# Spreading the side jobs of an attention loop anew over its 44 steps: one core, five engines, one table

## What is computed

```python
def xattn(x, context, Wq, Wk, Wv, Wo, bo):
    q, k, v = x @ Wq.T, context @ Wk.T, context @ Wv.T      # 16 heads of 16
    scores = einsum('bhqd,bhkd->bhqk', q, k) * SCALE
    probs = softmax(where(causal, scores, -inf))
    return (probs @ v) @ Wo.T + bo
x = x + tanh(g_xattn) * xattn(layernorm(x), ctx, ...)
x = x + tanh(g_ffn) * experts(layernorm(x), ...)            # top 128 of 512 tokens for each expert
```

## Time and profile before

| | |
|---|---|
| median of 3 runs | 1907.35 us (1906.61 to 1908.03) |
| the profiled execution | 1905.62 us |
| its span | 1903.9 us |
| PE busy | 1772.4 us, 93% |
| DVE, ACT, POOL busy | 1079.0 us, 930.5 us, 931.3 us |
| granted TensorE clock, mean | 0.975 |

### The profile page before, as it was taken

The page is one execution under the profiler, slowest core; times in us unless marked ns, Lnnn a source line. Parts: engine busy times, 40 slices in busy tenths (PEclk is TensorE's granted clock), DMA queues, the critical chain, the costliest instruction groups (busy, mean ns, idle before and its releaser), DMA issues.

```text
span 1903.9 us, 40685 instructions
## 1 busy us (share of the span) xinstructions
PE 1772.4 (93%) x12902; PEld 1017.8 (53%) x12902; DVE 1079.0 (57%) x3480; ACT 930.5 (49%) x1812; POOL 931.3 (49%) x1026
## 2 busy tenths in 40 slices
PE   3899999999999999935899999999899999999997
PEld 1355555555555555422465656565556565656565
DVE  2778888888888887737634343434343434343431
ACT  2466666666666666632334343434343434343332
POOL 6477777777777776543333232333322323333322
PEclk8899999999999999967999999999999999999999
DMA  5777777777777787347464644556736555555222
GB/s 161 163 172 188 189 188 188 188 188 188 188 188 188 188 189 168 81 132 177 100 132 84 120 98 89 98 90 122 123 61 121 100 89 98 89 97 82 48 34 23
DMA packets 408333, 247.85 MB, mean 130 GB/s; under 512 B 289303, under 2 KB 389759, under 8 KB 408191
## 3 DMA queue, kind: packets, MB, share of 16 engines
q1 hardware_dynamic: 383183, 212.39, 47.7%
q0 software_dynamic: 24576, 33.57, 11.3%
q10 hardware_dynamic: 432, 0.13, 0.0%
HBM read 118.63 MB, written 58.72 MB: 93 GB/s over the span
## 4 chain that ended last, share of the span: by engine, by line
PE 50%; DVE 3%; DMA 1%; issue 1%; ACT 0%; POOL 0%; SPq 0%; POOLq 0%; DVEq 0%
PE bank L1101 11%; PE bank L1102 11%; PE bank L1103 11%; PE bank L1117 6%; PE bank L1119 6%; PE bank L1118 6%; DVE h L1219 0%; DVE h L1222 0%; DVE top_at L1169 0%; ACT h L1147 0%; DVE work L1172 0%; DVE top L1167 0%; DMA rows<-tokens,row_now 0%; DMA out<-y,row_now 0%; POOL out L1067 0%
## 5 line engine op out<-in xcount | busy, mean ns | idle before, releaser
L1067 POOL DMA_INDIRECT out<-y,row_now x128 | 202.5, 1582 | 606.6 <-ACT y L1154 581.7
L681 DVE CUSTOM_DVE_ANT_0 masked<-bank,causal 128x128 bf16<-128x128 f32 (+3 forms) x1024 | 445.6, 484 | 69.1 <-PE bank L453 68.2
L565 ACT ACTIVATE prob<-bank 128x512 f32<-128x512 f32 x640 | 367.6, 596 | 158.1 <-PE bank L473 86.1
L1219 DVE TENSOR_TENSOR h<-bank,silu 128x512 f32<-128x512 f32 x256 | 176.4, 689 | 393.5 <-PE bank L1103 259.8
L1147 ACT ACTIVATE h<-h 128x512 bf16<-128x512 f32 x256 | 161.2, 630 | 345.4 <-DVE h L1219 328.5
L1117 PE MATMUL bank<-downT,h 128*128 128x256 bf16 x1024 | 279.1, 273 | 0.0
L1119 PE MATMUL bank<-downT,h 128*128 128x256 bf16 x1024 | 279.1, 273 | 0.0
L1118 PE MATMUL bank<-downT,h 128*128 128x256 bf16 x1024 | 279.1, 273 | 0.0
L1222 DVE TENSOR_TENSOR h<-h 128x512 bf16<-128x512 f32 x256 | 177.3, 692 | 179.7 <-ACT h L1147 175.5
L453 PE MATMUL bank<-ks,qs 96*128 96x128 bf16 (+3 forms) x1024 | 257.8, 306 | 21.0 <-DMA ks<-k_parts 11.4
L1101 PE MATMUL bank<-tokT,gateT 128*128 128x512 bf16 x512 | 195.0, 381 | 35.7 <-DMA tokT<-rows 28.9
(11 more groups left out here) (141 smaller groups left out, 2702.7 us busy)
## 6 DMA issues: line engine op xcount, KB each, us to landing
q_parts<-q_sb SPq DMA_DIRECT2D x64, 192.0 KB, 2.9
k_parts<-k_sb SPq DMA_DIRECT2D x64, 192.0 KB, 3.8
qs<-q_parts SPq DMA_DIRECT2D x64, 192.0 KB, 3.0
ks<-k_parts SPq DMA_DIRECT2D x64, 192.0 KB, 3.2
x_t<-in_x SPq DMA_DIRECT2D x16, 512.0 KB, 4.2
ctx_t<-in_ctx SPq DMA_DIRECT2D x16, 512.0 KB, 4.9
qs<-q_parts SPq DMA_DIRECT2D x64, 128.0 KB, 2.9
ks<-k_parts SPq DMA_DIRECT2D x64, 128.0 KB, 3.2
```

The source lines that it names most:

```text
L565: nc.scalar.activation(prob[:, gr % 2, h0:h0 + nh, POFF[tiles[0]]:POFF[tiles[0]] + w], sc_bank[SC_BANK[k]][:, 0:nh * w].rearrange("p (h w) ...
L681: last = nc.vector.tensor_tensor_reduce(masked[:, (gr * NMAX + k) % 2, part], max_bank[max_at(gr, k)][:, part], causal[:, T - w:T], 1.0, L ...
L1067: nc.gpsimd.indirect_dma_start(out_rows, bass.IndirectOffsetOnAxis(ap=row_now[:, par, c, s:s + 1], axis=0), y[:, c % 2, s, :], None, compu ...
```

## The change

The table `extra` in `steps` is written anew: the same jobs, with the same batch offsets, in other steps and in another order inside a step. Nothing else is changed: no instruction of the arithmetic, no shape, no buffer and no semaphore. `JOB_BANK` follows the order of the jobs, so a few jobs use the other of the two banks. Two of the 30 lines that go and 3 of the 36 that come, those that the prediction speaks of most:

```diff
@@ -85,36 +85,42 @@
 
 
     extra = {
...
-            9: [("pv", b - 1, 2, 3), ("xs", b - 2), ("ln2+", b - 2, 1)],
-            10: [("pv+", b - 1, 2), ("ln2+", b - 2, 0)]},
...
+            8: [("k", b + 1, 0, 0), ("ln2+", b - 2, 1), ("pv", b - 1, 2, 2)],
+            9: [("xs", b - 2), ("ln2+", b - 2, 0), ("pv", b - 1, 2, 3)]},
+        2: {1: [("pv+", b - 1, 2), ("k+", b + 1, 0), ("k", b + 1, 0, 1)],
...
```

More of the change, by code:

```diff
@@ L105, in steps @@
[L105 to L117, removed]
+        0: {0: [("mrow", b - 1, 3)],
+            1: [("ln1+", b + 1, 0), ("yt+", b - 1, 0), ("pv", b - 1, 1, 0), ("yt", b - 1, 0)],
+            2: [("xsplit", b + 1, 0)],
+            3: [("mt", b - 1, 3), ("ln1+", b + 1, 1), ("xturn", b + 1), ("xsplit", b + 1, 1), ("pv", b - 1, 1, 1), ("pv", b - 1, 1, 2)],
+            4: [("csplit", b + 1, 0), ("o", b - 2, 0, 0), ("o", b - 2, 0, 1), ("mt+", b - 1, 3)],
+            5: [("cturn", b + 1)],
+            6: [("o+", b - 2, 0), ("o", b - 2, 1, 0)],
+            7: [("csplit", b + 1, 1), ("o", b - 2, 1, 1), ("pv+", b - 1, 1), ("pv", b - 1, 1, 3), ("o+", b - 2, 1)],
+            9: [("yt", b - 1, 1)]},
@@ new lines, in steps @@
+        1: {0: [("qstack", b, 2), ("kstack", b, 2)],
+            1: [("yturn", b - 1, 0), ("yt+", b - 1, 1), ("mrow", b, 0), ("ysplit", b - 1, 0)],
+            2: [("mt", b, 0), ("mt+", b, 0), ("ln2", b - 2, 0)],
+            3: [("ln2", b - 2, 1), ("pv", b - 1, 2, 0), ("q", b + 1, 0, 0)],
+            4: [("q+", b + 1, 0), ("q", b + 1, 0, 1), ("q", b + 1, 1, 0)],
+            5: [("pv", b - 1, 2, 1)],
+            6: [("q", b + 1, 1, 1), ("kstack", b, 3), ("q+", b + 1, 1)],
+            8: [("k", b + 1, 0, 0), ("ln2+", b - 2, 1), ("pv", b - 1, 2, 2)],
+            9: [("xs", b - 2), ("ln2+", b - 2, 0), ("pv", b - 1, 2, 3)]},
@@ new lines, in steps @@
+        2: {1: [("pv+", b - 1, 2), ("k+", b + 1, 0), ("k", b + 1, 0, 1)],
+            2: [("mt", b, 1), ("mt+", b, 1)],
+            3: [("load", b + 2), ("pv", b - 1, 3, 0)],
+            4: [("k", b + 1, 1, 0), ("k", b + 1, 1, 1), ("k+", b + 1, 1)],
+            5: [("qstack", b, 3), ("yt", b - 1, 2), ("yt+", b - 1, 2), ("pv", b - 1, 3, 1)],
+            7: [("pv", b - 1, 3, 2), ("qstore", b + 1), ("vaug", b)],
+            8: [("pv+", b - 1, 3), ("mrow", b, 1), ("pv", b - 1, 3, 3), ("xt", b - 2, 0), ("xt+", b - 2, 0)],
+            9: [("res", b - 1), ("xt+", b - 2, 1)],
+            10: [("xt", b - 2, 1)]},
@@ new lines, in steps @@
+        3: {0: [("kstore", b + 1)],
+            1: [("mt+", b, 2), ("yt", b - 1, 3), ("yt+", b - 1, 3), ("qstack", b + 1, 0), ("mt", b, 2)],
+            3: [("ll+", b - 2), ("pv", b, 0, 0), ("ll", b - 2), ("v", b + 1, 0, 0), ("kstack", b + 1, 0)],
+            4: [("v+", b + 1, 0), ("v", b + 1, 0, 1), ("ln1", b + 2, 0), ("mrow", b, 2)],
+            5: [("ysplit", b - 1, 1), ("save", b - 2), ("lt", b - 2), ("yturn", b - 1, 1)],
+            6: [("kstack", b + 1, 1), ("v", b + 1, 1, 0), ("lt+", b - 2)],
+            8: [("v", b + 1, 1, 1), ("pv", b, 0, 1), ("v+", b + 1, 1)],
+            9: [("pv+", b, 0)],
+            10: [("ln1", b + 2, 1), ("pv", b, 0, 2), ("qstack", b + 1, 1), ("pv", b, 0, 3)]},
```

## The result

| | before | changed |
|---|---|---|
| median of 6 runs each, on the same chip | 1906.98 us (1905.86 to 1908.39) | 1873.25 us (1872.32 to 1877.36) |
| ratio, 95% interval | | 0.9827 (0.9814 to 0.9839) |
| span of the profiled execution | 1903.9 us | 1871.2 us |
| DVE, ACT, POOL busy | 1079.0, 930.5, 931.3 us | 1075.4, 932.2, 931.7 us |
| granted TensorE clock, mean | 0.975 | 0.974 |

The changed kernel is 33.7 us faster, 1.7%. The forecast was 1874. The other engines do the same work in the same time (DVE's and ACT's busy times move by 0.3% and 0.2%), so the gain lies in PE's time, above all in its waits, as argued. PE's own busy time can't be compared over the whole span: 64 of its records, all in the experts, are missing from the second trace. Whether the terms were right is another matter: several were not, and that they cancelled to within 1 us is luck.

What follows compares the result with a forecast made beforehand. PE sets the pace in the attention, with 3.0 us of waits a batch. 1905.6 less 36 over fifteen batches plus 2.5 at the start gives 1872, or 1874 on the scale of the median; range 1862 to 1900.

Steps and rivals of the forecast that it cites:

- three signs of being wrong: Period over 46.5, PE waiting for `ks` or `qs` in mid-attention, or the start losing over 5 us.
- PE's waits by starts: Attention: a batch of 47.7 us holds 44.7 us of PE work, so 3.0 us are waits; eleven places sum to 3.1.
- Rival 2: Attention: the busy row is right, PE idles only 2.5%, so the time is 1889 or more; chance 0.05.
- Period 45.2: Attention, per batch: 44.7 us of work, less 0.2 for `pv` pairs, plus 0.7 of new waits.
- g0 k5, 0.57 go: `sc` at g0 k5 waits 0.57 us for ACT behind an `ln1+` pair; moving `ln1+` to k1 and k3 removes it.
- g1 k8 to g2 k2: ACT makes `sc` late, 0.71 us, partly seen at `max`; `ln2+` in g1 k8, k9 and `pv+` at g2 k1 remove it.
- g2 k8 to g3 k2, 0.50 go: ACT is late for `sc` behind `xt+`, `pv+`, `xt+`; with PE's jobs moved, the 0.50 us wait goes.
- `pv` pairs, 0.09 each: Two pairs of `pv` now adjacent each save PE one entry of 0.09 us, 0.2 a batch.
- The SP chain has 0.9 of slack: `csplit`, `cturn`, stacks, `yturn`, `mrow` on SP's queue: `mrow` lands at 21.9, PE wants it at 22.8; slack unchanged at 0.9.
- Rival 4: Slower: late `csplit` makes SP's chain set g2; at 4 us of slip 1922; chance 0.07.
- 15 batches at the full 2.4: Attention: 2.4 to 2.5 us saved in each of fifteen batches at the full pattern, 36 us.
- The start loses 2.5: First 85 us, PE waits for DMA: SP's new order costs between 0 and 5 us, taken as 2.5.

Runs made afterwards that it cites:

- m_best: a_mrow with `yt` of group 1 at g0 k10 and `pv` 2.2 beside `pv` 2.3 at g1 k9; 1856.83 us, ratio 0.9736.
- b_ln12: b_ln2 with both `ln1+` pairs of group 0 also moved, to k1 and k3 from k2 and k4; 1904.16 us, ratio 0.9974.
- m_ln: a_mrow with `ln1+`, `ln2+` and `pv+` back where the kernel before has them; 1877.66 us, ratio 0.9837.
- b_ln2: Kernel before with only the `ln2+` pairs moved to g1 k8 and k9 and `pv+` to g2 k1; 1910.46 us, ratio 1.0011.
- m_lnk: m_ln with the first part of the `k` projection back in g2 k1 too; 1872.75 us, ratio 0.9817.
- a_mrow: Changed kernel with `mrow` of group 0 ahead of `yturn` and that of group 1 ahead of q's store on SP's queue; 1859.98 us, ratio 0.9746.
- b_k: b_ln12 with the first `k` part at g1 k8 instead of g2 k1 and `cturn` ahead of the stacks; 1902.12 us, ratio 0.9976.
- a_split: Changed kernel with `mt` of group 3 between the two `pv` of g0 k3 instead of ahead of them; 1873.66 us, ratio 0.9819.
- a_csplit: Changed kernel with the second `csplit` moved from g0 k7 to k9, delaying the SP transfers behind it; 1909.36 us, ratio 1.0006.

## Why the prediction was right, and where it was wrong

The direction is right, and so is the mechanism: waits of PE that go when the side jobs are moved. That the time is right to 1 us is luck, since terms of several us each were off and cancelled. One of its three signs of being wrong came true: PE waits for `qs` in the middle of the attention. By its own steps:

- *PE's waits by starts*, 3.0 to 3.1 a batch: 3.18, and 47.7 as period: 47.75. Right, and the largest part of the gain, 1.84 of 2.45 a batch, is these waits. Rival 2, the busy row, is refuted: it capped the gain at 1889, and the changed kernel ran 1873, m_best 1857. The Trainium skill, "Perfetto Trace Analysis", Identifying the Most-Contended Engine, holds matmul busy time for no measure of headroom. This case agrees: 97.5% busy hid 3.2 us of waits in 47.75, 6.7%.
- *Period 45.2*: 45.3. Right as a sum. Its two parts are each off by half a microsecond and cancel: waits left 0.7 forecast, 1.34 measured; work saved 0.2 forecast, 0.6 measured.
- *g0 k5, 0.57 go*: 0.57 to 0.16 at g0 k4. The size is right, the cause only half: b_ln12 shows that moving `ln1+` alone removes the wait, and m_ln that the new places of the other jobs remove it as well, with `ln1+` where it was. In the new table the move of `ln1+` wins nothing; the 0.15 at g0 k4 stands only with it.
- *g1 k8 to g2 k2, "0.71 go" by the split of `ln2+`*: the wait went (0.69 to 0.36, and the 0.36 is the `mrow`), but **the cause was mis-booked**. b_ln2 shows that the split alone wins nothing. The step that failed is reading a wait of `max` for DVE as part of ACT's; the trace named DVE there. `ln2+` with `pv+` is nonetheless worth 17.7 us in the new table once the k part stands in g1 k8 (m_ln). There the k part without it costs 4.9 us (m_ln against m_lnk), and both together win 12.8 (m_lnk to a_mrow); `ln2+` without the k part wasn't run in this table. In the old table both together win nothing (b_k), so they also need what else the new table has there.
- *g2 k8 to g3 k2, 0.50 go*: 0.51 to 0.13, and that is an `mrow`. Here too a part was put to ACT that stood elsewhere: 0.17 of it was a wait of `mt`, which needs DVE's maxima and a bank, not ACT's `prob`. *Group 1's start 0.43*: 0.49. *Banks 0.40, g0 k0 0.33 go*: none left. Right; these were not tried one by one.
- *`pv` pairs, 0.09 each*: **mis-sized**; a_split gives 0.24 for one, so two would be 0.48 of the 0.6. I had priced the entry and not the exit and the matmul that otherwise starts between.
- *The SP chain has 0.9 of slack*: **wrong**, and already as a reading of the kernel before. `sc` needs both transfers of an `mrow`, and the second is issued 0.6 after the first (two take 1.18); 342.37 + 0.6 + 1.8 is 344.8, and `sc` of g2 k0 started at 345.36, so 0.6 us were left, by the timeline of PE in the kernel before:

```profile
345.36 0.22 PE L470 MATMUL bank<-qs,ks 128*128 128x128 bf16 x1
```

  In the changed kernel `csplit` ended 12.85 us after g0 k0 (forecast 11.8), as the timeline of POOL shows, 324.45 + 1.16 - 312.76:

```profile
324.45 1.16 POOL L809 TENSOR_TENSOR c_nat<-ctx_t,c_nat 128x512 bf16<-128x512 f32 x1
```

  `cturn` followed 0.2 later, and `mrow` was issued at 20.9 (forecast 19.3). Its landing was as forecast, 1.7 us in batch 6. The median over all groups from 300 to 700 us did rise from the 1.8 of the earlier trace rows to 2.1, because the `mrow` of group 1 now takes longer, 3.1 in batch 6 (window 342.5 to 345.5):

```profile
qs<-m_sb SPq DMA_DIRECT2D x2, 4.0 KB, 3.1
```

  Rival 4's mechanism is real, at a small part of its size: 0.3 to 0.5 us in a steady batch, 8 us in a_mrow without the clock, and it hides every saving ahead of g2 k0. a_csplit is rival 4 played out.
- *15 batches at the full 2.4*: **wrong**. Batches 1 to 5 gave 1.66 each. It is the same chain: batches 4 and 5 gave 2.7 each, batches 1, 2 and 3 only 1.3, 1.0 and 0.6. At g2 k0 or g3 k0 PE waits in them for `mrow`, and in batch 3 for the stack of k too, 1.3, 1.5 and 2.3 us more than in a steady batch. a_mrow won 3.7 in these five batches. Why the transfers of batch 2 land later is open.
- *The start loses 2.5*: it won 0.5, with a half-clock stretch in it that cost about 4. *Experts 0*: 0.7. The two sides come to nearly the same: forecast -36 + 2.5 = -33.5, measured -31.5 in batches 1 to 15, -0.5 at the start and -0.7 in the experts, -32.7.

## What to carry to other kernels

In a loop of in-order engines a move is worth what is late next, so price it together with the next waiter: `ln2+` was worth nothing alone in the old table and 18 us in the new one. When small savings on the full engine vanish, look for a wait for a tiny transfer (4 KB here) and count back what stands ahead of it in its queue; two swaps in SP's order gave 13 us, 8 of them without the clock, more than any further move of arithmetic. Take waits from starts, place by place, and before trusting a sum test one term alone: a right total can stand on two wrong terms.
